# Storing the last two tiles of a streamed residual kernel in pieces of 64, 60, 4, 120 and 8 partitions

## The reference

```python
# x: (128, 128, 1024), itok_B_0_7: (128,) int32 below 8, L0_cond_weights: (8, 128, 128)
def _L0_cond_ref(x, subjects, weights):
    w = weights[subjects]
    out = jnp.einsum('bct,bcd->bdt', x, w)
    return out
x = x + _L0_cond_ref(x, itok_B_0_7, L0_cond_weights)
```

## Time and profile before

| | us |
|---|---|
| median of 3 timed runs | 325.82 |
| lowest and highest of them | 325.64, 326.04 |
| the profiled execution | 326.13 |
| span of the profiled execution, first to last instruction | 324.2 |
| VectorE busy | 238.5 |
| TensorE busy | 238.1 |
| GpSimd busy | 201.5 |
| ScalarE busy | 70.4 |

### The profile page before, as it was taken

How to read it: one execution, slowest core, us unless ns; L and a number is a source line. 1 busy time by engine, 2 the same in 40 slices (tenths; PEclk the granted TensorE clock), 3 DMA queues, 4 the chain that set the end, 5 groups by cost and what they waited for, 6 DMA issues and landing times.

```text
span 324.2 us, 4021 instructions
## 1 busy us (share of the span) xinstructions
PE 238.1 (73%) x1024; PEld 106.2 (33%) x1024; DVE 238.5 (74%) x208; ACT 70.4 (22%) x81; POOL 201.5 (62%) x197
## 2 busy tenths in 40 slices
PE   0599999999977877876867768768677687686700
PEld 0244444444433333332332323323233233233300
DVE  3089999999987787686776876867768768677630
ACT  5122322222222112122122121221221212212200
POOL 0377878888875665665755756657557566574320
PEclk9999999999999999999999999999999999999975
DMA  7999999999999999999999999999999999999993
GB/s 284 425 409 415 424 428 423 430 425 428 426 428 428 425 432 425 428 427 427 428 426 431 425 429 426 427 428 425 432 425 429 426 429 426 428 429 422 430 426 165
DMA packets 18968, 134.82 MB, mean 416 GB/s; under 512 B 2065, under 2 KB 2578, under 8 KB 2578
## 3 DMA queue, kind: packets, MB, share of 16 engines
q1 hardware_dynamic: 9744, 67.64, 49.8%
q10 hardware_dynamic: 9218, 67.11, 49.0%
HBM read 67.63 MB, written 67.11 MB: 416 GB/s over the span
## 4 chain that ended last, share of the span: by engine, by line
DMA 63%; PE 28%; ACT 2%; issue 1%; DVE 1%; POOLq 0%; DVEq 0%; ACTq 0%; POOL 0%; SPq 0%
DMA out<-x_ring 39%; PE product L189 28%; DMA x_ring<-x 23%; DMA weight_halves<-weights 1%; ACT weight_bank L130 1%; ACT weight_bank L131 1%; POOLq L154 0%; DVEq L37 0%; DVE x_ring L91 0%; DVE x_ring L89 0%; ACTq L116 0%; POOL weight_ring L155 0%; SPq L71 0%; ACT crossed L111 0%; POOLq L155 0%
## 5 line engine op out<-in xcount | busy, mean ns | idle before, releaser
L189 PE MATMUL product<-x_ring,weight_ring 64*128 64x512 f32 x1024 | 238.1, 603 | 68.9 <-DMA x_ring<-x 55.3
L161 POOL TENSOR_TENSOR x_ring<-crossed,x_ring 64x1024 f32<-64x1024 f32 x64 | 150.6, 2352 | 90.5 <-ACT crossed L111 90.5
L189 PEld LDWEIGHTS product<-x_ring,weight_ring 64*128 64x128 f32 x1024 | 106.2, 188 | 200.1 <-issue 192.4
L89 DVE TENSOR_TENSOR x_ring<-product,x_ring 64x1024 f32<-64x1024 f32 x64 | 77.9, 1217 | 65.7 <-PE product L189 64.5
L111 ACT COPY crossed<-product 64x1024 f32<-64x1024 f32 x64 | 64.3, 1004 | 234.2 <-PE product L189 209.7
L90 DVE TENSOR_TENSOR x_ring<-product,x_ring 64x1024 f32<-64x1024 f32 x64 | 78.6, 1228 | 0.8
L91 DVE TENSOR_TENSOR x_ring<-product,x_ring 64x1024 f32<-64x1024 f32 x64 | 78.5, 1226 | 0.9
L155 POOL COPY weight_ring<-weight_bank 64x256 f32 x128 | 50.8, 396 | 18.3 <-issue 12.2
L98 DVE COPY weight_bank<-weight_halves 64x128 f32<-64x128 f32 x8 | 1.8, 219 | 4.8 <-DMA weight_halves<-weights 4.7
L130 ACT COPY weight_bank<-weight_halves 64x128 f32<-64x128 f32 x8 | 2.4, 303 | 2.0 <-DMA weight_halves<-weights 2.0
L131 ACT COPY weight_bank<-weight_halves 64x128 f32<-64x128 f32 x8 | 2.4, 299 | 0.1
## 6 DMA issues: line engine op xcount, KB each, us to landing
x_ring<-x SPq DMA_DIRECT2D x64, 1024.0 KB, 18.6
out<-x_ring ACTq DMA_DIRECT2D x64, 1024.0 KB, 31.5
weight_halves<-weights SPq DMA_DIRECT2D x1, 512.0 KB, 3.9
subject_row<-subjects ACTq DMA_DIRECT2D x1, 0.5 KB
```

The costliest lines, as they stand in the source:

```text
L89: dve.tensor_tensor(x_ring[LOW, slot, 0, :], low[LOW, :], x_ring[LOW, slot, 0, :], add)
L161: pool.tensor_tensor(x_ring[HIGH, slot, 1, :], crossed[HIGH, slot % 2, :], x_ring[HIGH, slot, 1, :], add).then_inc(joined, 1)
L189: last = pe.matmul(product[slot % PRODUCTS][a][:, cols], weight_ring[half, slot, r, :], x_ring[half, slot, r, cols], start=r == 0, stop=r ...
```

## The change

A table `PIECES` names, for the last two tiles alone, ranges of partitions. `store` issues one DMA for each range, all on the slot's semaphore and all behind the same two waits. Tile 62 is stored as partitions 0 to 63, 64 to 123 and 124 to 127; tile 63 as 0 to 119 and 120 to 127. All other tiles keep one DMA of 128 partitions. The closing wait expects 16 for each piece.

```diff
+PIECES = {-2: ((0, 64), (64, 124), (124, 128)), -1: ((0, 120), (120, 128))}
...
-            def store(tile, slot):
+            def store(tile, slot, pieces=((0, C),)):
                 act.wait_ge(summed, tile + (PRODUCTS + 1))
                 act.wait_ge(joined, tile + 1)
-                act.dma_start(out_of_tile[bass.ds(tile, 1)], x_ring[:, slot, :, :]).then_inc(x_out[slot], DMA_INC)
-
-            def step(tile, slot):
+                for begin, end in pieces:
+                    act.dma_start(out_of_tile[bass.ds(tile, 1), begin:end, :],
+                                  x_ring[begin:end, slot, :, :]).then_inc(x_out[slot], DMA_INC)
+
+            def step(tile, slot, pieces=((0, C),)):
 
                 act.wait_ge(joined, tile - 1)
                 cross(tile, slot)
-                store(tile - 1, (slot - 1) % SLOTS)
+                store(tile - 1, (slot - 1) % SLOTS, pieces)
...
             for slot in range(REST):
-                step(LAPS * SLOTS + slot, slot)
-            store(TILES - 1, REST - 1)
+                step(LAPS * SLOTS + slot, slot, PIECES.get(slot - 1 - REST, ((0, C),)))
+            store(TILES - 1, REST - 1, PIECES[-1])
             for slot in range(SLOTS):
-                act.wait_ge(x_out[slot], DMA_INC * (LAPS + (slot < REST)))
+                last_pieces = len(PIECES.get(slot - REST, (0,))) if slot < REST else 0
+                act.wait_ge(x_out[slot], DMA_INC * (LAPS + last_pieces))
```

## The result

The changed kernel takes 329.71 us (median of 8 runs, 327.55 to 330.17) beside 326.04 us for the kernel before in the same session (8 runs, 325.64 to 326.46): a ratio of 1.0104 with a 95% interval of 1.0082 to 1.0127. The forecast was 323.1 us. The time moved the other way, and beyond the range. The runs now scatter over 2.6 us, those of before over 0.8. The profiled execution took 330.04 us with a span of 328.3.

The account below looks back on a forecast made before the run. A DMA stream at some 426 GB/s, ended by one late engine, bounds the kernel. Taking 3.7 us off that engine moves the data end from 323.1 to 320.4: 325.82 - 2.7 = 323.1 us, range 322.4 to 327.2.

Parts of the forecast that it names:

- What bounds the kernel: Whole run: a DMA stream at some 426 GB/s; at the end one late engine works alone for the last 2.9 us.
- How a store is shared out: Tiles 62 and 63: rows are cut evenly over up to 16 engines; 60 and 120 rows use 15, leaving one out.
- counts of 18, 17 and 16: Last two tiles: packets on the fifteen other engines; four engines have 18, four 17, seven 16.
- If that is the late one: End of the stores: if the left-out engine is the late one, it ends at 319.4 us and is no longer last.
- 3.7 us off: Last two tiles: the left-out engine has 4 packets where it had 16, so 12 x 0.309 us less.
- the second rival: End: the left-out engine is not the late one; 0, 0.31 or 0.62 us more, most likely 325.9 us; chance 0.16.
- Packets of half-partition stores at 0.309 us: Pieces of tiles 62 and 63: the forecast priced each packet at 0.309 us, as in whole stores.
- The first rival: Pieces of tiles 62 and 63: halves are slow as engines share a way out; 327.2 us, 0.4% slower; chance 0.26.
- 2.7 us: Last two tiles: the gain forecast; slow halves turn its sign where an engine loses more than this.
- The Trainium skill's port rule: 64-row stores: 64 neighbouring partitions reach 8 of 16 ports, 196 GB/s; the first two pieces take some 2.8 us more.
- Issue and small packets at nothing: ScalarE's three more DMAs, 0.34 to 0.38 us each, hidden by the backlog; added small packets at most some 0.05 us.
- The range: Whole kernel's time: from 322.4 us, a little under the 3.0 us bound, up to 327.2 us for slow halves.

Follow-up runs that it names:

- lower-half: Against the kernel before, tile 63 stored as two DMAs of 64 rows, both read from partitions 0 to 63: 329.01 us, ratio 1.0097.
- upper-half: Against the kernel before, tile 63 stored as two DMAs of 64 rows, both read from partitions 64 to 127: 326.20 us, ratio 1.0011.
- the three early tiles: Against the kernel before, tiles 2, 3 and 4 each stored as 112 rows and four pieces of 4 rows: 328.05 us, ratio 1.0048.

## Why the prediction was wrong

- **What bounds the kernel**: right. The stream fills the DMA engines, and the end hangs on one late engine, alone and at its full rate. Before and after show the same picture.
- **How a store is shared out**: right. 58 closings show that 60 and 120 rows run on 15 engines, and the late engine's 4, 8 and 1 packets are the even shares. (The fifteen others keep 16 packets, not 12; the counts of 18, 17 and 16 that follow are right.)
- **"If that is the late one"**: this is the first step that failed. The engine left out is not the late one; it keeps 17 packets. The prediction saw that no row names it, and counted with it all the same; that the late engine is a fixed one did not make it the one left out. The sum's 3.7 us off turned into 0.3 us on, just the second rival's price for 17 packets. The Trainium skill's rule on the engine count ("DMA: Bandwidth & Descriptors", "Why a DMA increments its semaphore by 16 and not by 1") agrees with every count here. Its remark on engines 7 and 15 ("Latency and other measured facts") is no guide here: counted by that rule, the late engine is the fifth, number 4. As a best guess the page ties the remark to DMAs issued from GpSimd, which this kernel does not have; the prediction passed over that.
- **Packets of half-partition stores at 0.309 us**: the second step that failed. Of the bounds the lower was taken, because loads and stores together ran at 426 GB/s. That evidence was of whole stores alone and said nothing of pieces. Measured, the rate fell to 311 to 360 GB/s, some 0.38 us for a packet on the mean.
- **The first rival** named the mechanism and the direction but put the price in the wrong place. It charged the sharing to the 15 engines and let their time in hand pay. But the price fell on the one engine with nothing in hand: the others reached the pieces while it was still on tiles 60 and 61, and 3.4 us went on tile 61. The two lower-half and upper-half kernels show this apart from all else. So it turned the sign at once, not beyond 2.7 us, and 327.2 was too low.
- **The Trainium skill's port rule** ("SBUF — State Buffer", "Door 1: The DMA port swizzle (why [64,N] ≈ [32,N])") spoke against the change. At the end of the kernel the direction agrees (311 to 360 GB/s beside 426). A long stream does not bear it out: 424 GB/s with all stores in halves beside 426.
- **Issue and small packets at nothing**: right in the sum. Four stores by columns in place of two cost 0.0%, 32 more small packets included. But one issue of the changed kernel took 1.15 us where 0.34 to 0.38 was counted; it was hidden all the same, since the last piece left ScalarE at 311.1 us and the first engines reached tile 62 about 314.
- **The range** ended at 327.2 because it held the late engine and the sharing as alternatives. They came together, and the second acted on the first.

Even with the right engine left out the gain would have been doubtful: others would have read its rows through the same way while it was still using it. That is argued from the lower-half kernel; no run left out the right one.

## What to carry to other kernels

Before work is moved off a late DMA engine, find out which one it is, for instance by pieces of 4, 5, 6 and 7 rows on the last tile, counted in the trace. Store with all 128 partitions near the end of a DMA-bound kernel: pieces that cover half of them slow each other, and what counts is whether they also slow the engine that ends last. If a store must be cut, cut its columns: that cost nothing here.

## What was not expected

Stores of half the partitions, 64 tiles long, run at 424 GB/s; put behind whole stores they cost more. Kernels with such pieces scatter by 2 to 4 us from run to run (327.55 to 330.17 for the changed kernel, 325.86 to 330.12 for the three early tiles). Of 92 runs of the kernel before, 89 lie within 1.8 us (325.06 to 326.78), and three went up to 327.14, 327.71 and 328.00. And the late engine is 4.5 us late in the kernel before without being slow at the end: its last packets take 0.309 us like all others. What makes it late was not tried.
